# Encoded state transposed by the DMA queue, borders of the stages reordered: a two-network graph kernel on one core

## The reference, cut to what matters

```
h = relu(layernorm(x));  h = relu(h @ enc_w1.T + b1) @ enc_w2.T + b2        # encoder: the encoded state
for w in conv_w (5 layers):                                                 # gated graph network
    agg = segment_sum((h @ w)[src], dst)
    h = GRU(agg, h)
x = x + sigmoid(relu(relu(h) @ dec_w1.T + b) @ dec_w2.T + b)
h = relu(layernorm(x))                                                      # second network, 2 spmm
v = dinv[row] * dinv[col];  h = relu(spmm(v, h) @ W1.T + b1);  x = x + (spmm(v, h) @ W2.T + b2)
```

## Time and profile before

| what | us |
|---|---|
| median of the runs | 750.3 |
| the profiled execution: time / span | 750.97 / 748.8 |
| PE busy (matmul) | 722.3 |
| DVE busy | 334.2 |
| ACT busy | 314.6 |
| POOL busy | 45.7 |

### The profile page before, as it was taken

How to read it: one execution, slowest core, us unless ns; L and a number is a source line. 1 busy time by engine, 2 the same in 40 slices (tenths; PEclk the granted TensorE clock), 3 DMA queues, 4 the chain that set the end, 5 groups by cost and what they waited for, 6 DMA issues and landing times.

```text
span 748.8 us, 9901 instructions
## 1 busy us (share of the span) xinstructions
PE 722.3 (96%) x4074; PEld 395.5 (53%) x4074; DVE 334.2 (45%) x675; ACT 314.6 (42%) x461; POOL 45.7 (6%) x55
## 2 busy tenths in 40 slices
PE   3899999999999999999999999999999999999997
PEld 2566666445444444444444444444444545567986
DVE  7999998434013332122331222656644721124322
ACT  3978777655334444234452334432446421211000
POOL 6320000000000000000000000120011310000000
PEclk9999999999999999999999999999999999999999
DMA  5120000743202233021240212620002000000100
GB/s 164 26 75 2 1 1 1 132 83 60 40 1 47 52 54 59 1 48 38 45 83 0 48 37 38 105 71 2 1 0 103 1 1 1 1 1 2 38 27 28
DMA packets 78795, 28.40 MB, mean 38 GB/s; under 512 B 70340, under 2 KB 77893, under 8 KB 78618
## 3 DMA queue, kind: packets, MB, share of 16 engines
q1 hardware_dynamic: 77786, 26.93, 17.1%
q0 software_dynamic: 240, 0.66, 0.3%
q10 hardware_dynamic: 720, 0.13, 0.1%
HBM read 8.03 MB, written 2.60 MB: 14 GB/s over the span
## 4 chain that ended last, share of the span: by engine, by line
PE 85%; DVE 8%; ACT 3%; DMA 2%; SPq 1%; POOL 1%; issue 1%; ACTq 0%; DVEq 0%
PE PSA L1199 34%; PE PSA L1417 8%; PE PSA L1282 7%; PE PSA L1362 5%; PE PSA L1145 4%; PE PSA L1213 3%; PE PSA L1222 3%; PE PSA L1215 3%; PE PSA L1217 3%; PE PSA L1221 3%; PE PSA L1224 3%; DVE CT L836 2%; PE PSA L1350 2%; ACT AT L1524 1%; PE PSA L1338 1%; DVE stat L801 1%
## 5 line engine op out<-in xcount | busy, mean ns | idle before, releaser
L1199 PE MATMUL PSA<-AT,H 128*128 128x512 fp8e3 (+1 forms) x1472 | 276.2, 347 | 1.0 <-DMA H<-H 0.5
L1199 PEld LDWEIGHTS PSA<-AT,H 128*128 128x128 f16 x1472 | 126.8, 98 | 152.6 <-issue 13.0
L1040 DVE SCALAR_TENSOR_TENSOR rS<-PSA,bias,rS 128x512 f32<-128x512 f32 (+1 forms) x35 | 23.9, 682 | 266.4 <-ACT rS L1591 266.4
L1591 ACT ACTIVATE rS<-PSA,bias 128x512 f32<-128x512 f32 (+1 forms) x35 | 22.1, 632 | 199.6 <-PE PSA L1221 199.6
L836 DVE TENSOR_TENSOR CT<-CT 128x2048 bf16<-128x2048 bf16 x80 | 91.3, 1206 | 0.1
L1524 ACT ACTIVATE AT<-PSA 128x1000 fp8e3<-128x1000 f32 (+1 forms) x79 | 74.3, 1000 | 23.1 <-PE PSA L1145 23.1
L1498 ACT ACTIVATE CTL<-AT 128x3125 fp8e3<-128x3125 fp8e3 (+1 forms) x25 | 69.9, 2797 | 0.0
L1362 PE MATMUL PSA<-CT,H 128*128 128x512 fp8e3 (+1 forms) x336 | 65.5, 351 | 1.2 <-POOL H L746 1.2
L1417 PE MATMUL PSA<-AT,CT 128*128 128x256 f16 x576 | 64.9, 273 | 0.7 <-DVE AT L1012 0.7
L1417 PEld LDWEIGHTS PSA<-AT,CT 128*128 128x128 fp8e3 x576 | 55.5, 98 | 7.4 <-DVE AT L1012 0.9
L1282 PE MATMUL PSA<-AT,H 128*128 128x512 fp8e3 x250 | 59.0, 379 | 0.0
(11 more groups left out here) (171 smaller groups left out, 658.3 us busy)
## 6 DMA issues: line engine op xcount, KB each, us to landing
AT<-scale_scratch SPq DMA_DIRECT2D x1, 1562.5 KB, 6.4
H<-in_x SPq DMA_DIRECT2D x1, 1536.0 KB
out<-AT SPq DMA_DIRECT2D x12, 128.0 KB
comb_scratch<-CT SPq DMA_DIRECT2D x1, 960.0 KB, 4.7
comb<-comb_scratch SPq DMA_DIRECT2D x5, 192.0 KB, 3.0
H<-yS SPq DMA_TRANSPOSE x48, 2.5
H<-in_x SPq DMA_DIRECT2D x1, 512.0 KB, 4.8
CT<-AT SPq DMA_TRANSPOSE x25, 4.0
```

The lines of the kernel that those rows point to most:

```text
L1199: last = nc.tensor.matmul(bank[:, 0:w], H16[:, l % 2, t, h, :], AT3[:, t, n0:n0 + w], start=(t == 0 and h == 0), stop=(t == T - 1 and (h = ...
```

## The change

Five things change.

1. The encoded state goes to node-major form as the states of the layers do. ACT writes the high half from HT into S16[:, 0] (same batch 2s+2), SP transposes it into H16 by DMA; DVE writes the low half from HT into S16[:, 1], now in batch 2s+3, and SP transposes that. Semaphore `encoded_moved` counts both (32 a chunk); high and low half s wait for chunk s-1 to be moved, since S16 is one buffer. PE's transposes L1187 are gone. `aggregate_part` waits for the DMAs. The store of the combined weights comes behind the 14 transposing DMAs in SP's order.
2. The parts are placed about one batch later (30 in the loop), and banks for q = 1 and q = 2 are exchanged.
3. PE does two matmuls on `wtop` before anything else.
4. At the border, three of PE's partial sums each change place, and POOL does its first three low halves before the fourth power.
5. At the end, the check's reduction goes behind output 4 and the flag behind output 16, the check's matmul behind tile 9; the last expansion and the last two projections come earlier by a tile.

More of the change, by code:

```diff
@@ L205, in gnn_kernel @@
         STARTED = len(TILES)
+        CHECKED = 4
         EARLY = 3
@@ L568, in _ @@
             sp.wait_ge(window_bank_free, NGR)
+            sp.wait_ge(small_set, 5)
             def columns(t):
@@ L857, in low_encoded @@
             def low_encoded(s):
-                t0, nt = CH[s]
-                k = rows(t0)
+                n0, w = CH[s][0] * P, width(s)
                 dve.wait_ge(encoded_hi, s + 1)
-                nc.vector.scalar_tensor_tensor(
-                    H16[0:k, 0, t0:t0 + nt, 1, :], PS[EB][0:k, 0:nt * F].rearrange("p (t f) -> p t f", t=nt), S0,
-                    H16[0:k, 0, t0:t0 + nt, 0, :], ALU.mult, ALU.subtract).then_inc(encoded_lo, 1)
+                if s >= 1:
+                    dve.wait_ge(encoded_moved, 32 * s)
+                nc.vector.scalar_tensor_tensor(S16[:, 1, 0:w], HT[:, n0:n0 + w], S0, S16[:, 0, 0:w], ALU.mult, ALU.subtract
+                                               ).then_inc(encoded_lo, 1)
             dve.wait_ge(small_set, 1)
@@ L997, in decoded_tail @@
                         biased_output(c)
[L999 to L1006, removed]
                 for u in range(2 * FG):
@@ L1013, in decoded_tail @@
                                                    ALU.mult, ALU.add).then_inc(output_ready, 1)
+                    if u == CHECKED:
+                        link(nc.vector.tensor_reduce(chk[0:P, 2:3], Z16[:, :, 0, :], AX.XY, ALU.max, apply_absolute_value=True))
+                        nc.vector.tensor_scalar(chk[0:P, 2:3], chk[0:P, 2:3], LIMIT * S0, None, ALU.is_gt).then_inc(check_ready, 1)
+                    if u == FG + CHECKED:
+                        dve.wait_ge(check_summed, 1)
+                        nc.vector.tensor_scalar(flag_f[:, 0:1], PS[RB][0:1, 0:1], float(E), None, ALU.not_equal)
+                        nc.vector.tensor_copy(flag_f[:, 1:2], PS[RB][0:1, 1:2])
+                        link(nc.vector.tensor_copy(flag_f[:, 2:4], PS[RB][0:1, 2:4]))
+                        link(nc.vector.tensor_reduce(flag_f[:, 4:5], flag_f[:, 0:4], AX.X, ALU.add))
+                        nc.vector.tensor_copy(flag[:, :], flag_f[:, 4:5]).then_inc(flag_ready, 1)
                     if u == FG - 1:
@@ L1179, in encoder @@
                     nc.tensor.matmul(PS[EA][:, 0:w], enc1, aggS[:, 0:w], start=True, stop=True).then_inc(enc1_product, 1)
-                if off % 2 == 1 and s >= 1:
-                    t0, nt = CH[s - 1]
-                    pe.wait_ge(state_encoded, s)
-                    if s >= 2:
-                        pe.wait_ge(encoded_lo, s - 1)
-                    k = rows(t0)
-                    for j in range(nt):
-                        last = nc.tensor.transpose(PS[EB][0:k, j * F:(j + 1) * F],
-                                                   HT[:, (t0 + j) * P:(t0 + j) * P + k], ident[:, :])
-                    last.then_inc(encoded_transposed, 1)
             def aggregate(bank, w, n0, l, ready=None, between=None):
@@ L1272, in aggregate_part @@
                 if g == 0 and q == 1:
+                    pe.wait_ge(rows_found, 2)
+                if g == 0 and q == 2:
                     pe.wait_ge(enc1_relu, NC)
-                if g == 0 and q == 2:
-                    pe.wait_ge(encoded_lo, NC)
                 if g == 0 and q == 3:
@@ L1442, in _ @@
                 tile_sum(u, 20, 24)
-            pe.wait_ge(late_ones_set, 2)
-            pe.wait_ge(check_ready, 1)
-            nc.tensor.matmul(PS[RB][0:1, 0:4], onesL[:, 0:1], chk[:, 0:4], start=True, stop=True).then_inc(check_summed, 1)
             pe.wait_ge(projected_packed, 64)
@@ L1452, in _ @@
                 tile_ends(u)
+                if u == CHECKED + STARTED:
+                    pe.wait_ge(late_ones_set, 2)
+                    pe.wait_ge(check_ready, 1)
+                    nc.tensor.matmul(PS[RB][0:1, 0:4], onesL[:, 0:1], chk[:, 0:4], start=True, stop=True).then_inc(check_summed, 1)
                 if u == STARTED:
@@ L1568, in encoder @@
                 if off % 2 == 1 and s >= 1:
[L1569 to L1576 removed]
+                    n0, w = CH[s - 1][0] * P, width(s - 1)
+                    act.wait_ge(state_encoded, s)
+                    if s >= 2:
+                        act.wait_ge(encoded_moved, 32 * (s - 1))
+                    nc.scalar.activation(S16[:, 0, 0:w], HT[:, n0:n0 + w], ACT.Copy, scale=S0).then_inc(encoded_hi, 1)
             def aggregated(q):
@@ L1648, in _ @@
                         act.wait_ge(state_ready, q - 1)
+                        if c == 2 and l == 0:
+                            act.wait_ge(encoded_moved, 32 * NC)
                         if c - 2 == NC - 1 and l >= 1:
```

13 lines of the change are left out of this document (3 added, 10 removed).

## The result

The changed kernel took 753.1 us (median of 21 runs, 752.28 to 754.22), the kernel before beside it 751.32 (21 runs, 750.07 to 753.16): ratio 1.0022, 95% interval 1.0015 to 1.0028, or +1.8 us where +0.8 was forecast (751.1 us, from the 750.3 that the kernel before had in its first three runs). In its profiled execution the span was 749.7 us and the time 752.73. There is a surprise in these numbers: from one profiled execution to the other the span grew by 0.9 us and the time by 1.8. What lies outside the span (first to last instruction) was 2.17 us before and is 3.03 now, and it is so in every run that has its span on record: 2.0 to 2.2 in 49 of the kernel before, 2.83 to 3.19 in 21 of the changed one.

A forecast was written before the change was run, and what follows sets the result against it. DVE was taken to bound the window loop up to batch 18, PE only behind it. Terms +2.7 - 0.1 - 0.6 - 1.2 = +0.8 us on the 750.3 median gave 751.1 us, range 748.0 to 754.0.

The forecast's parts named there:

- (a): Window loop: DVE's earlier low halves wait for ACT's high halves, 2.1 us against 0.4; batch 18's tiles 1.7 us later.
- (b): Window loop: shifted partial sums put small part (0,6) in batch 18, where PE then waits; +1.0 us, ends 0.4 and 1.3.
- start: Two f32 matmuls before 5 us may remove DVE's 0.34 us wait for a sample matmul; -0.1 us, ends -0.3 and +0.1.
- border: 570 to 612 us: PE's reordered sums fill its waits, POOL's earlier low halves delay DVE; -0.6 us, ends -2.0 and +0.3.
- end: Check reduction into the output loop, last chunk projected a tile earlier, output tile 5 starts sooner; -1.2 us, ends -1.5 and -0.5.
- the forecast as worked out: The main case, DVE setting the time up to batch 18: 751.1 us, own range 749.5 to 752.2, chance 0.45.
- part 1: Encoded path in the window loop, transposes moved from PE to transfers: +2.7 us together, ends -1.9 and +5.5.
- rival C: Window loop: ACT stands further behind, DVE's waits for it sum to 3.5 us; 752.7 us, chance 0.17.
- Rival A: Window loop: DVE isn't the bound, PE's removed transposes pay in full, -3.8 us; 746.5 us, chance 0.08.
- The transfers: Window loop: 14 transposing DMAs land 2.5 us after issue, hidden; 5 us between low and next high half, no wait.
- the chain: Border: DVE, POOL and ACT work ending with the packing that PE's last wait there needs; +1.2 us later.
- rival B: PE idles about 2.0 us before windows 14 at 64 to 66 us, clock falls again; +1.7, 752.8 us, chance 0.14.

The follow-up runs named there:

- the second half alone: Kernel before with everything but the encoded path: start matmuls, border order on PE and POOL, check inside the output loop; 747.93 us, ratio 0.996.
- the PE orders alone: Kernel before with PE's border order and the whole end change, POOL's low halves as before, no start matmuls; 748.05 us, ratio 0.9956.
- the start alone: Kernel before with only the two f32 matmuls at the start added; 750.85 us against 751.77, ratio 0.9988.

## Why the forecast came out as it did

| step | forecast, us | measured, us | by |
|---|---|---|---|
| (a) DVE waits for ACT, batch 18 late | +1.7 | +2.3 | 75.70 to 78.00 |
| (b) parts shifted, small part later | +1.0 | +0.7 | gate matmul plus one part, less (a) |
| start | -0.1 | 0 | one-hots begin 0.09 us earlier, which is in the first row |
| layers, not touched | 0 | -0.2 | gate matmul to chunk 3's bias, less one part |
| border | -0.6 | -0.9 | between the marks |
| end | -1.2 | -1.3 | between the marks |
| last tiles, not touched | 0 | +0.2 | tile 5 to the end of the span |
| outside the span | 0 | +0.9 | 2.17 to 3.03 |
| sum | +0.8 | +1.8 | of the unrounded terms; the profiled executions: 750.97 to 752.73 |

The total is 1.0 us above the forecast, and that is the term outside the span, which was held to be constant. Inside, (a) was 0.6 too small, (b), the border and the end together 0.7 too large; that these cancel is luck. In absolute time 751.1 us was forecast and 753.1 measured: 1.0 of the difference is the change, and 1.0 is the kernel before, whose median was 751.32 over 21 runs and not 750.3. The 753.1 lies in the range of 748.0 to 754.0, but above the 752.2 that was the upper end for the forecast as worked out. So the path was right; that the time falls in the range owes something to the range's width.

Three sums of the forecast don't come out: the waits listed under (a) add up to 1.9 or 2.0 us and not 2.1; its ends of 3.5 and 1.3 us give +4.4 for part 1, not +5.5; and rival C, with waits of 3.5 in place of 2.1, gives 752.5 and not 752.7. None changes the argument.

**DVE, not PE, sets the time to batch 18: right, and shown.** The kernel with the transposes put back costs nothing, and the chain of the changed kernel is DVE's. Rival A, PE's time saved in full, needed 746.5 us and is out; it would also have needed windows 18 at 74 us or earlier.

**(a), right in kind, short in size.** The waits came where they were put: low 0 0.22 us (forecast 0.2), low 2 0.22 (0.1 to 0.2), low 5 1.42 (1.1), low 6 0.56 (0.3). They make 2.4 us against 0.4 before, 2.0 of the 2.3 by which batch 18 is late. The rest is in the same waits. In a closed row DVE's operations begin before the one ahead has ended (one of 0.15 us at 49.49 in the kernel before, the next at 49.56), and one that waits loses this too. Low 3 has no bracket in the timeline, but it begins 0.23 us behind the start of that same short operation (50.06 and 50.29), so 0.16 of its 0.2 came as well. Putting the low half back shows the cause: windows 18 are 2.67 us earlier, DVE's wait is gone, and it is worth 3.0 us in all. Rival C named 3.5 us of such waits for 752.7; the time is near that, the waits are not, so it is not what happened.

**(b)** was read as a difference of two marks; with the low halves put right the same difference against the second half alone, which has no encoded path, is 1.0 us, the forecast's number (131.57 + 1.73 - 75.33 against 132.03 - 75.10). Moving the parts forward takes 2.1 us back. So the table of parts leaves room unused in front of DVE.

**The transfers: no wait in the changed kernel, as forecast.** I had 5 us between low s-1 and high half s against 2.5 us of landing. With the low half one batch later, ACT waits 1.0 us in two waits, still hidden; with the transfers doubled 3.2 us in four, and DVE behind it. The margin is thinner than 5 against 2.5 made it look.

**The border: the rule was right, and the gain a little larger.** All three DVE operations beside POOL's low halves were held: 1.59 and 1.64 us for additions of 0.69, and 1.26 for the tensor_scalar that takes 0.43 alone. The last one decides between the two values of the forecast (-0.6 and -2.0), and it is the row that the rule for two-port modes foretold: the Trainium skill (SBUF — State Buffer, "SBUF: two separate sides") has a DVE operation take the shared pair if it has two SBUF inputs or runs in a two-port mode, and a one-input f32 tensor_scalar can only be held under the second half of it. The trace agrees. The price of the move is also shown without the rule: the PE orders alone gain 1.7 us, with POOL moved 0.9. What I summed as +1.2 for the chain came as 0.8.

**The end** came as worked out: the packing issued at 686.73, or 684.78 if the 1.95 us is taken off by which the mark before it is later (forecast: 684.65), PE without a wait in front of ZP, 0.61 us left in front of tile 5 in place of 1.58 in three.

**The clock.** The dip after batch 6 came again, as in the earlier trace rows, and in the profiled execution no second one near 65 us, where PE was idle 2.21 us. So rival B is out for this execution, but its mechanism is real. In the kernel with the transfers doubled PE was idle 2.69 us there, and the granted clock then was 0.50 from 68 to 70 us; a part of 1.89 us took 3.41:

```profile
67.12 1.31 PE L1163 MATMUL PSA<-CT 128*128 128x125 bf16 x16 [2.69 <-DVE CT L849]
68.23 3.41 PE L1290 MATMUL PSA<-AT,H 128*128 128x512 fp8e3 x8
```

And 4 of the 21 runs of the changed kernel have a mean granted clock of 0.988, lower than the others' 0.990 to 0.999, and spans of 751.0 to 751.2 us against 749.2 to 750.7. A second dip in these is likely; no trace of them was kept. Stretches of the changed kernel (last three columns: granted clock, DMA share, GB/s):

```profile
36.00:38.00 2.00, 0.00 (x0) 0.00 (x0) 2.00 (x3) 0.84 (x2) 1.14 (x1) 1.00 0.27 51
38.00:40.00 2.00, 1.43 (x14) 1.43 (x15) 2.00 (x6) 0.37 (x1) 0.00 (x0) 0.54 0.08 15
...
64.00:66.00 2.00, 0.53 (x8) 0.40 (x5) 2.00 (x3) 1.98 (x3) 0.00 (x0) 1.00 0.38 74
66.00:68.00 2.00, 1.26 (x18) 1.15 (x19) 2.00 (x3) 0.58 (x1) 0.00 (x0) 1.00 0.77 65
```

**What the forecast did not have at all** is the step outside the span, half of the measured loss. It was the one place where the time of the profiled execution and its span were taken to differ by a constant.

## What to carry to other kernels

Before you take work from an engine, ask in that stretch who waits for whom: here PE's transposes ran in PE's waits for DVE, and freeing them moved nothing until the parts were moved into the gap. When an operand moves to another engine's output, look whether the consumer still comes after the producer with time to spare; one batch too early cost 3.0 us of 750 here, and one changed condition gave it back. And compare the time with the span: a change can cost where no instruction of the trace is.

## What was not expected of the hardware

- The encoded path with its fourteen transposing transfers of 128x512 f16 from SBUF to SBUF in the window loop goes with 0.9 us more outside the span: 1.99 to 2.20 us in 49 runs of the kernel before and all of the five others without it, 2.83 to 3.32 in all 60 runs of the seven with it. Fourteen plain transfers from DRAM don't do it (2.04), and twice as many transposing ones don't add to it (3.14). The kernel before has transposing transfers too, 48 in the layers, so it isn't their mere presence. What it is stays open; no run here varied how few, or when the first of them, is enough, or left them out of the path.
- The granted clock was 0.50 in some 2 us or more between 38 and 42 us in the profiled executions of five kernels, and 1.00 there in eight others, with PE idle for 2.08 to 2.69 us before it in either group, and with or without the start matmuls in either. The 16 window matmuls of batch 6 took 1.77 us in the kernel before and 1.13 in the start alone.
- Two matmuls on an otherwise idle PE at 1.58 us change the clock that runs show: 44 of the 71 runs with them have a mean granted clock of 0.988 to 0.993, none of the 74 without them is below 0.995 (in the start alone 7 of 11, in the kernel before beside it none of 21). In four of the eight profiled executions with them the granted clock falls to 0.50 between 8 and 10 us, with PE idle from about 7 to 12, and stays there until 18 us or later. The first 16 window matmuls, near 15.8 us, took 1.86 us in these, but also in the kernel before, where the clock reads 1.00 there.
- The lock between DVE and POOL holds both ways: POOL's three low halves took 4.01 us beside the additions, and 3.38 beside the short operations.
